# Experts' attention: three bfloat16 parts and one head at a time, against two float32r parts and two heads in two row tiles

## The reference, cut to what matters

```python
h = _ln(jax.nn.relu(x @ ew1 + eb1) @ ew2 + eb2, eg, ebeta)      # D = 256
qkv = h @ aiw + aib
q, k, v = jnp.split(qkv, 3, axis=-1)                             # NH = 16 heads of DH = 16
attn = jax.nn.softmax(jnp.einsum('bhqd,bhkd->bhqk', q, k) * SCALE, axis=-1)
o = jnp.einsum('bhqk,bhkd->bhqd', attn, v)
h = o @ aow + aob
hf = _lstm_dir(h, wif, whf, bf)       # starts with the products h @ Wi
...
```

## Time and profile before

| | us |
|---|---|
| median of 3 runs | 5220.26 (5219.8 to 5220.53) |
| the profiled execution, its own time | 5218.64 |
| its span | 5216.8 |
| TensorE busy | 5014.9 (96%) |
| its weight loads busy | 3521.8 (68%) |
| VectorE busy | 4108.0 (79%) |
| ScalarE busy | 2403.0 (46%) |
| GpSimd busy | 1160.7 (22%) |

### The profile page before, as it was taken

One profiled execution on the slowest core, in us unless ns is written; L12 is line 12 of the kernel. 1 busy time (PEld: TensorE's weight loads), 2 busy tenths in 40 slices (PEclk: granted clock), 3 DMA queues, 4 the chain that ended last, 5 costly groups with the idle time before them and its releaser, 6 DMA issues. The chain is left out here.

```text
span 5216.8 us, 258340 instructions
## 1 busy us (share of the span) xinstructions
PE 5014.9 (96%) x108736; PEld 3521.8 (68%) x108736; DVE 4108.0 (79%) x19260; ACT 2403.0 (46%) x8371; POOL 1160.7 (22%) x5143
## 2 busy tenths in 40 slices
PE   7989799999999996999999999999999999998997
PEld 4656333333333335998999999999999999994444
DVE  3857666666666648999999999999999999992225
ACT  2734565555555534444444444444444444442334
POOL 0000011111111102333333333333333333330000
PEclk9989899999999998999999999999999999999998
DMA  0024654544535431101111011101110111102120
GB/s 15 1 99 145 135 90 90 112 90 96 126 74 131 90 139 50 41 18 39 41 25 41 17 41 25 41 17 41 25 41 25 33 41 25 41 1 88 52 67 11
DMA packets 378834, 302.26 MB, mean 58 GB/s; under 512 B 146153, under 2 KB 357609, under 8 KB 373002
## 3 DMA queue, kind: packets, MB, share of 16 engines
q1 hardware_dynamic: 378430, 298.20, 23.9%
HBM read 179.14 MB, written 119.01 MB: 57 GB/s over the span
## 5 line engine op out<-in xcount | busy, mean ns | idle before, releaser
L1439 PE MATMUL bank<-lparts,lstate 128*32 128x256 bf16 x98304 | 2697.2, 273 | 56.1 <-PEq L1382 46.8
L1439 PEld LDWEIGHTS bank<-lparts,lstate 128*32 128x32 bf16 x98304 | 2454.1, 97 | 299.8 <-issue 47.6
L1450 DVE STREAM_TRANSPOSE ltz<-bank 128x256 f32<-128x256 f32 x2048 | 921.2, 450 | 9.0 <-PE bank L1439 4.1
L1514 ACT ACTIVATE ltc<-lgc 128x16 f32<-128x16 f32 x2049 | 443.0, 216 | 1030.0 <-DVE lgc L1471 1030.0
L1528 POOL TENSOR_TENSOR wh<-lgate,ltc 128x16 f32<-128x16 f32 x2052 | 471.2, 230 | 1799.8 <-ACT ltc L1514 1728.8
L1255 ACT ACTIVATE wh<-bank 128x512 f32<-128x512 f32 x1024 | 549.7, 600 | 481.0 <-PE bank L1042 480.9
L1167 DVE TENSOR_REDUCE bnegmax<-bank 128x1 f32<-128x512 f32 x1024 | 654.0, 682 | 128.5 <-PE bank L1024 128.0
L1509 ACT ACTIVATE lgate<-lz 128x48 f32<-128x48 f32 x2048 | 498.6, 243 | 522.6 <-DVE lz L1461 522.6
L1535 POOL COPY ltz<-wh 128x64 f32<-128x64 f32 x2048 | 603.2, 295 | 0.0
L1457 DVE TENSOR_TENSOR lhalf<-ltz 128x128 f32<-128x128 f32 x2048 | 583.1, 285 | 10.5 <-POOL ltz L1535 6.3
L1104 PE MATMUL bank<-xT,bw 128*128 128x512 f32 x1024 | 489.4, 602 | 2.7 <-DVE bzs L1188 1.9
(11 more groups left out here) (215 smaller groups left out, 4317.0 us busy)
## 6 DMA issues: line engine op xcount, KB each, us to landing
zx<-bzs SPq DMA_DIRECT2D x32, 2048.0 KB, 7.3
wh<-zx SPq DMA_DIRECT2D x64, 1024.0 KB, 7.4
qk<-eparts SPq DMA_DIRECT2D x96, 256.0 KB, 2.8
bqp<-qk SPq DMA_DIRECT2D x192, 128.0 KB, 4.8
bkp<-qk SPq DMA_DIRECT2D x192, 128.0 KB, 8.0
hs<-wh SPq DMA_DIRECT2D x32, 512.0 KB, 5.8
cmemT<-hs SPq DMA_DIRECT2D x32, 512.0 KB, 4.7
vx<-evx SPq DMA_DIRECT2D x16, 544.0 KB, 4.1
```

The lines of the kernel that those rows point to most:

```text
L1439: last = nc.tensor.matmul(bank[x][32 * q:32 * q + 32, 0:256], top[:, x, e, k].rearrange("p m r -> p (m r)"), parts[:, way, g, k, n, e, q], ...
L1450: nc.vector.transpose(tz[:, x].rearrange("p (n w) -> p n w", w=SLOT)[:, :, 0:32], bank[x][:, 0:256].rearrange("p (n c) -> p n c", n=BLOCKS ...
L1514: nc.scalar.activation(tc[:, x], gc[:, x, 1], ACT.Tanh).then_inc(tanhed[x], 1)
```

## The change

In the encoding, queries and keys become two parts: high is ScalarE's copy rounded to float32r (F32R), low is VectorE's difference qk - high in f32. The second copy and the second subtraction go. d["qk"] holds two f32 parts in place of three of bf16.

In the attention a step is a pair of heads, 128 steps. The pair lies in the two halves of the partitions, 51 rows each: 16 of high with high, 16 of high with low, 3 for the maxima, 16 of low with high. SP loads quarters (two pairs, twelve transfers) into a staging tile, and GpSimd copies every pair from there into qp and kp, converted to float32r (copy_pair), five pairs ahead. Each score and each transposed score is two matmuls, one on partitions 0 to 50 and one on 64 to 114. A score group goes to banks 0 and 1, one for each head, and waits until both reductions of the group before are done. The maxima of a pair are turned by four full matmuls of 128 columns. The 24 pieces of an earlier slab are spread evenly, three a step (piece_of_earlier). SP's list is rewritten, and the recurrence's weights are loaded ahead of the last store of slab 14.

The removed lines are left out where the functions printed above show them.

```diff
-        rest = core.sb(ctx, "erest", [P, 2, KH, S])
-        parts = core.sb(ctx, "eparts", [P, 2, 2, 3, KH, S], BF16)
+        high = core.sb(ctx, "ehigh", [P, 2, 2, KH, S], F32R)
+        low = core.sb(ctx, "elow", [P, 2, 2, KH, S])
...
+                def low_part(b, side):
+                    dve.wait_ge(high_done[side], b + 1)
+                    nc.vector.tensor_tensor(low[:, b % 2, side], qk[:, side], high[:, b % 2, side].bitcast(F32), ALU.subtract
+                                            ).then_inc(low_done[side], 1)
...
+                def high_part(b, side):
                     act.wait_ge((q_kept, k_kept)[side], 2 * b + 2)
                     if b >= 2:
...
+                        act.wait_ge(qk_out[side][b % 2], b // 2 * 32)
+                    nc.scalar.activation(high[:, b % 2, side], qk[:, side], ACT.Copy).then_inc(high_done[side], 1)
...
+HALF = P // 2
+HIGH_ROWS, MAX_ROWS, LOW_ROWS = 2 * DH, 3, DH
+SCORE_ROWS = HIGH_ROWS + MAX_ROWS + LOW_ROWS
+STAGED = 4
 RING = 8
...
+        qp = core.sb(ctx, "bqp", [P, NH // 2, S], F32R)
+        kp = core.sb(ctx, "bkp", [P, NH // 2, S], F32R)
+        staged = core.sb(ctx, "bstaged", [P, STAGED, 2, S])
...
+                def load_pairs(quarter):
+                    slab, first = divmod(2 * quarter, STEPS)
+                    for side, rows in ((0, ((0, 0), (0, DH), (1, HIGH_ROWS + MAX_ROWS))),
+                                       (1, ((0, 0), (1, DH), (0, HIGH_ROWS + MAX_ROWS)))):
+                        for part, at in rows:
+                            src = d["qk"][slab, side, part].rearrange("(p two r) n -> two r p n", two=2, r=DH)
+                            for half in range(2):
+                                lo = half * HALF + at
+                                sp.dma_start(staged[lo:lo + DH, quarter % 2 * 2:quarter % 2 * 2 + 2, side],
+                                             src[half][:, first:first + 2]).then_inc(staged_in[quarter % 2], 16)
...
+                sp.wait_ge(blank, 2)
+                for quarter in range(2):
+                    load_pairs(quarter)
                 load_values(0)
...
                 load_out_weights(0)
                 load_columns(0)
                 for way in range(2):
                     load_in_weights(0, way)
...
+                for quarter in range(2, 4):
+                    sp.wait_ge(copied, 4 * (quarter - 1))
+                    load_pairs(quarter)
+                for j in range(PAIRS + 1):
+                    slab, at = divmod(j, STEPS)
+                    quarter = j // 2 + 4
+                    if j % 2 == 0 and 2 * quarter < PAIRS:
+                        sp.wait_ge(copied, 4 * (quarter - 1))
+                        load_pairs(quarter)
+                    if at == 1 and slab >= 2:
+                        store_products(slab - 2, 0)
+                        if (slab - 2) % B == B - 1:
+                            sp.wait_ge(z_mm, NH * (slab - 2) + BLOCKS)
+                            load_in_weights((slab - 1) // B, 0)
+                    if at == 3:
+                        if slab < SLABS - 1:
+                            if slab > 0:
+                                sp.wait_ge(valued, NH * slab)
+                            load_values(slab + 1)
+                        if slab >= 2:
+                            store_products(slab - 2, 1)
+                            if (slab - 2) % B == B - 1:
+                                sp.wait_ge(z_mm, NH * (slab - 1))
+                                load_in_weights((slab - 1) // B, 1)
+                                load_columns((slab - 1) // B)
+                    if at == 6 and slab >= 1 and slab % B == 0:
+                        sp.wait_ge(a_mm, KH * slab)
+                        load_out_weights(slab // B)
+                store_products(SLABS - 2, 0)
+                sp.wait_ge(valued, NH * SLABS)
+                sp.dma_start(core.wh[:], d["wh"]).then_inc(wh_in, 16)
+                store_products(SLABS - 2, 1)
+                for way in range(2):
+                    store_products(SLABS - 1, way)
...
                 def score(j, qt):
...
+                    if qt == 0:
+                        pe.wait_ge(copied, 2 * (j + 1))
+                    if BT * j + qt > 0:
+                        pe.wait_ge(maxed, 2 * (BT * j + qt))
+                    for half in range(2):
+                        rows = slice(half * HALF, half * HALF + SCORE_ROWS)
+                        nc.tensor.matmul(bank[half][:], qp[rows, j % STEPS, qt * P:(qt + 1) * P], kp[rows, j % STEPS],
+                                         start=True, stop=True).then_inc(scored, 1)
 
                 def turn_maxima(j):
                     pe.wait_ge(part3, j + 1)
                     if j > 0:
...
+                        pe.wait_ge(rows_kept, 2 * j)
                     for qt in range(BT):
...
+                        last = nc.tensor.matmul(bank[5][:, qt * P:(qt + 1) * P], maxparts[:, j % 2, qt], ident16[:],
+                                                start=True, stop=True)
                     last.then_inc(rows_mm, 1)
 
                 def score_t(j, kt):
...
+                    n = 2 * (BT * j + kt)
                     if kt == 0:
...
+                        pe.wait_ge(rows_kept, 2 * (j + 1))
+                    if n >= 2:
+                        pe.wait_ge(exped, n - 1)
+                    for half in range(2):
+                        rows = slice(half * HALF, half * HALF + SCORE_ROWS)
+                        nc.tensor.matmul(bank[2 + (n + half) % 3][:], kp[rows, j % STEPS, kt * P:(kt + 1) * P],
+                                         qp[rows, j % STEPS], start=True, stop=True).then_inc(scored_t, 1)
 
...
+                    pe.wait_ge(exped, 2 * (BT * (2 * g + 1) + kt + 1))
...
+                def piece_of_earlier(j, place):
+                    slab, piece = earlier(j, place)
+                    if piece < 0:
+                        return
+                    if piece < BT:
+                        turn_values(slab, piece)
+                    elif piece < BT + KH:
+                        turn_divided(slab, piece - BT)
+                    elif piece < BT + 2 * KH:
+                        project(slab, piece - BT - KH)
+                    else:
+                        for k in range(KH):
+                            product(slab, piece - BT - 2 * KH, k)
+
                 pe.wait_ge(zeroed, 3)
                 for j in range(LAST_STEP):
...
+                    if j < PAIRS:
                         score(j, 0)
+                    if 2 <= j < PAIRS + 2:
+                        score_t(j - 2, 2)
+                    piece_of_earlier(j, 0)
+                    if j < PAIRS:
                         score(j, 1)
...
+                    if 2 <= j < PAIRS + 2:
+                        score_t(j - 2, 3)
+                    if 1 <= j < PAIRS + 1:
+                        turn_maxima(j - 1)
+                    piece_of_earlier(j, 1)
+                    if j < PAIRS:
                         score(j, 2)
...
+                    if 1 <= j < PAIRS + 1:
+                        score_t(j - 1, 0)
+                    if j >= 3:
+                        for kt in (0, 1) if j % 2 == 1 else (2, 3):
+                            if j >= 3 + kt // 2:
+                                values((j - 3 - kt // 2) // 2, kt)
+                    if j < PAIRS:
                         score(j, 3)
...
+                    if 1 <= j < PAIRS + 1:
+                        score_t(j - 1, 1)
+                    piece_of_earlier(j, 2)
...
                 def largest(j, qt):
...
+                    for half in range(2):
+                        dve.wait_ge(scored, 2 * (BT * j + qt) + half + 1)
+                        if j >= STEPS and qt == 0 and half == 0:
+                            dve.wait_ge(part3, j - STEPS + 1)
+                        nc.vector.tensor_reduce(negmax[:, j % STEPS, half, qt:qt + 1], bank[half][:], AX.X, ALU.max,
+                                                negate=True).then_inc(maxed, 1)
 
...
+                    columns_of = maxparts[:, j % 2].rearrange("p t (h c) -> p h t c", h=2)
+                    parts = [columns_of[:, :, :, HIGH_ROWS + n] for n in range(MAX_ROWS)]
+                    pool.wait_ge(maxed, 2 * BT * (j + 1))
...
+                def copy_pair(j):
+                    quarter = j // 2
+                    pool.wait_ge(staged_in[quarter % 2], PIECES_IN * (quarter // 2 + 1))
+                    if j >= STEPS:
+                        pool.wait_ge(scored_t, 2 * BT * (j - STEPS + 1))
+                    for side, to in ((0, qp), (1, kp)):
+                        nc.gpsimd.tensor_copy(to[:, j % STEPS], staged[:, j % STAGED, side]).then_inc(copied, 1)
+
+                nc.gpsimd.memset(staged[:, :, 1], 1.0).then_inc(blank, 1)
+                for j in range(COPY_AHEAD):
+                    copy_pair(j)
+                pool.wait_ge(zeroed, 3)
+                for j in range(PAIRS):
```

(69 more changed lines are left out.)

231 lines of the change are left out of this document (58 added, 173 removed).

## The result

The changed kernel takes 5295.35 us (median; 5294.4 to 5301.42) beside 5220.4 of the kernel before (5219.8 to 5222.93): ratio 1.0144, interval 1.0132 to 1.0156. It is slower by 75 us, 1.4%, where I had forecast 29 us faster. The profiled executions have spans of 5293.3 and 5216.8 us.

The account below looks back on a forecast made before the run. TensorE's instruction list was taken as the bound. Encoding -2, steady slabs -59, slab 0 +12, start +16 and end +4 gave -29 us on 5218.6: 5190 us, range 5155 to 5362.

Parts of the forecast that it names:

- three slots of 1.83: Pairs with transposes: three score groups, each at least 1.83 us from the next through score, two reductions and back.
- One pass, row tiles beside each other: Scores: float32r takes one pass and two row tiles run together, 0.22 us a couple, 14.2 us a slab instead of 27.8.
- A: Rival, scores: float32r needs two passes, 0.43 us a couple, 170 us more in all, 5360; chance 0.15.
- B: Rival, scores: the two row tiles don't run beside each other, +9 us a slab, 5330; chance 0.07.
- Changes of tile shape: TensorE, attention: 64 changes a slab instead of 32, at 0.12 to 0.20 us each, 1.27 us in a three-product pair.
- rival C: TensorE, attention: tile changes and weight loads dearer, rounded weights loading like f32; +28 us, 5218, up to 5250; chance 0.16.
- Turning pairs: The two pairs with transposes in each slab: 8.7 and 8.9 us, part of a 79.9 us slab against 84.0.
- Slab 0: First attention slab, without pieces: a pair takes 8.5 us where two heads took about 6.6; +12 us.
- The start: Attention start: GpSimd copies five pairs before its first split, the fifth behind SP's queued loads; +16 us, ends +5 and +20.
- GpSimd, SP, VectorE in the slabs: Steady slabs: GpSimd's copies stay hidden, SP's loads land in time, VectorE at 52 us a slab stays below 80.
- The end: Last slab: its ninth product waits 7 us for a delayed store, free banks take back about 3; +4 us.
- Encoding: Encoding stage: two last subtractions no longer stand ahead of the last store, -2 us; dropped copies otherwise worth nothing.

Follow-up runs that it names:

- e6: Changed kernel plus two full-array bf16 matmuls of zeros at each of three places in pairs 1 to 10, nothing taken away: 5287.07 us.
- e4: Changed kernel plus one full-array bf16 matmul between score and turned couple, at two places in each of pairs 2 to 127: 5326.46 us.
- e2: Changed kernel with GpSimd copying two pairs instead of five ahead of its first split, catching up later: 5285.36 us.
- e1: Changed kernel with each half's score matmul waiting only for the reduction of its own bank: 5260.06 us.
- e7: Changed kernel with per-bank score waits, two copies ahead of the first split, and full-array filler matmuls in pairs 1 to 10: 5242.54 us.
- e8: Changed kernel with the value product ahead of the first turned couple in slot 2 of each pair: 5295.23 us.
- e12: Changed kernel with per-bank waits, two copies first, values first only in pairs 0 to 10 and turning pairs, no fillers: 5204.26 us, 0.9964 of the kernel before.
- e10: Changed kernel with per-bank waits, two copies first, fillers, values first in pairs 0 to 10, turning pairs and behind the last: 5205.4 us, 0.9966 of the kernel before.
- e9: Changed kernel with per-bank waits, two copies first, fillers in pairs 0 to 10, values first everywhere, 18 matmuls before the first score: 5261.42 us.

## Why the prediction was wrong, point by point

- **What failed, in one sentence**: where TensorE does not fill its time, in slab 0 (8.5 us a pair) and in the turning pairs ("three slots of 1.83", 8.7 + 8.9), the sum had every step at its full-clock length, and the granted clock fell there. The second failed term is the price of a change of tile shape. The spans differ by 76.5 us, 105.5 more than the forecast's -29: 29.5 in start and slab 0, 71.5 in the steady slabs, 4.5 outside them.
- **One pass, row tiles beside each other** (against rivals A and B): right. Couples start 0.33 us apart, 0.22 of it streaming, the two heads of one mostly 3 to 4 ns apart.
- **Changes of tile shape**: the mechanism right, the term too small. Back to the scores 0.20 (forecast 0.15), into values 0.18 (0.12), into products 0.22 (0.20), and 0.12 of first weights behind the maxima, which I had at nothing: together 4 x 0.05 + 0.06 + 2 x 0.02 + 0.12 = 0.42, near the 0.4 by which a pair is over (10.80 for 10.4; 10.55 for 10.1 where projections stand in it). Six such pairs are 2.3 us a slab, 32 over 14 slabs. This is rival C at the size that it was given (+28), and its condition held: weights at 186 to 190 ns. The Trainium skill (TensorE: Matmul & The Clock Gate, Weight-path perf modes) says that the fast load is not for FP32; the trace shows float32r on that side.
- **Turning pairs**: 9.48 and 11.23 for 8.7 and 8.9 in the slab shown, 9.48 and 9.21 where the clock held. The fourteen whole slabs (copies at 743.86 to 1934.88) take 85.07 us in the mean, 5.2 over the forecast of 79.9. Of these 2.3 are the changes above; 1.1 are waits that were too short in the sum at full clock too (slots of 1.85 to 2.11 us for 1.83, the value slot 3.5 for 3.2 to 3.4); and 1.8 are the low clock, since a slab in which it held takes 83.28. Over fourteen slabs these are 32, 15 and 25 us, which is the steady slabs' miss, 12.5 + 59 = 71.5.
- **Slab 0**: +12 forecast. The first group copy and the next four groups hold start and slab 0 together: +57.5, against 28. A pair takes 12.0 and not 8.5, at a granted clock of 0.60; with fillers added and the same waits it takes 10.0 at 0.89, and 9.2 where it lies wholly at 2.4 GHz (e6). If the fillers hide in the waits, as the added matmuls of e4 do, about 2.8 of the 3.5 us are the clock's; this is an estimate.
- **The start**: +16 forecast, first turned maxima 10.6 later (614.05 against 603.42). The copies took 0.56 us apart and not 1.1, and the fifth waited 11.7 us for its load. The size was wrong, the queue that I named was the cause: e2 gives 10 us back.
- **GpSimd, SP, VectorE in the slabs**: right, nobody waits for them but the score groups for the reductions.
- **The end**: +4 forecast. The ninth product of the last slab did not wait; additions are 1.72 us apart before and behind it. **Encoding** -2: no gain to be seen, the first load of the attention is issued at 583.05 us before and at 584.70 after.
- The rivals left out the one that came: 5295 lies above C's own range and below B's. Nearest was C, which gives 28 us. That the stated range (to 5362) holds the time is luck: it reached so far only because of A and B, whose mechanisms are not in the trace.

That the clock costs time of its own is shown by the changed kernel itself, whose turning pair takes 9.21 or 11.23 us with the same work and waits, and by the two runs that only add work and make a stage shorter, e6 for slab 0 and e4 for the turning pairs. e1, e7, e8 and e12 take waits away and raise the clock at once. In the steady slabs the two can be told apart, as done above for e1 and e8; in slab 0 they were not. The Trainium skill (TensorE: Matmul & The Clock Gate, A second HAM failure mode: psum-queue depth-cycling) tells of small idle times between groups of matmuls, from cycling through banks, that make the clock swing. I did not weigh it in the forecast. The trace agrees as far as it goes: idles of 0.4 to 0.75 us stand ahead of the drop shown above. But they stand in the slab without a drop as well.

## What to carry to other kernels

Halving the work of a saturated TensorE doesn't only give its share back: where the other engines' waits come out from under it, the granted clock can fall, and each wait grows with it. So read a forecast's idle slots one by one, and for any stretch where TensorE no longer fills its time work the sum at 1.2 GHz too. The cure here was the wait and its place in the order (per buffer, behind a long block). Dummy work gave 8 us while the waits stood (e6) and nothing once they were gone (e10 beside e12); and a cure that helps one kind of step must be checked in the others, as values first was.

## What the runs showed that I had not expected

- A couple of float32r matmuls of 51 rows and 512 columns costs 0.22 us beside its first weights, as one bf16 matmul, but its weights load like f32, 186 to 190 ns.
- A round trip from row tiles to one full-array bf16 matmul and back costs 0.37 us where nothing waits, 0.31 beside the matmul, and nothing where TensorE waits for a reduction anyway (e4).
- Adding two matmuls to every pair made the group with the turning pairs 1.64 us shorter in the slabs where the clock then held (e4).
- 18 full-array matmuls ahead of the first score gave 2.4 GHz at 591.7 us and lost it at 598.5 (e9); nothing that I tried kept it through the first pairs, where TensorE has only scores to do; e10 kept it to 612.8, with 24 of them and more between the scores.
